# A graph network kernel: x loaded ahead of the weights, VectorE's order in the preamble changed, seven projection steps put ahead of the edge loop

## The reference, cut to what matters

```python
h = jnp.maximum(_layernorm(x, axis=-1), 0.0)          # x: 512 x 512
# layer 0, on h:
z = _ln(h, ln1_g, ln1_b)
q = (z @ Wq + bq).reshape(L, H, D)                    # L = 512 nodes, H = 8 heads, D = 64
k = (z @ Wk + bk).reshape(L, H, D)
v = (z @ Wv + bv).reshape(L, H, D)
scores = einsum('ehd,ehd->eh', q[row], k[col]) * scale + bias     # one row for each edge
m = segment_max(scores, row); p = exp(scores - m[row])
alpha = p / segment_sum(p, row)[row]
out = segment_sum(alpha[:, :, None] * v[col], row)
x = h + out.reshape(L, C) @ Wo + bo
# then a feed-forward part of the layer, and three further layers
```

## Time and profile before

| what | value |
|---|---|
| median of 3 runs | 392.35 us (392.17 to 392.61) |
| the profiled execution's own time | 392.51 us |
| its span in the profile | 391.0 us |
| TensorE busy | 371.8 us, 95% of the span |
| VectorE busy | 312.3 us, 80% |
| ScalarE busy | 171.6 us, 44% |

### The profile page before, as it was taken

One profiled execution on the slowest core, in us unless ns is written; L12 is line 12 of the kernel. 1 busy time (PEld: TensorE's weight loads), 2 busy tenths in 40 slices (PEclk: granted clock), 3 DMA queues, 4 the chain that ended last, 5 costly groups with the idle time before them and its releaser, 6 DMA issues.

```text
span 391.0 us, 5100 instructions
## 1 busy us (share of the span) xinstructions
PE 371.8 (95%) x1782; PEld 280.6 (72%) x1782; DVE 312.3 (80%) x660; ACT 171.6 (44%) x287; POOL 4.2 (1%) x19
## 2 busy tenths in 40 slices
PE   2889999999999999999989999999999999999994
PEld 2545566666657888887768788887578878787883
DVE  5889999999948689897876978499875778488356
ACT  5664665563145233343568623361363531125320
POOL 4000000000000000000000000000000000000000
PEclk9999999999999999999999999999999999999999
DMA  7602444343126000067400321400420032000002
GB/s 234 259 1 70 148 155 148 106 140 121 58 80 218 1 3 0 2 216 268 161 2 1 123 94 31 183 2 0 134 83 0 3 106 108 3 0 0 2 6 101
DMA packets 16360, 32.92 MB, mean 84 GB/s; under 512 B 1360, under 2 KB 1488, under 8 KB 16336
## 3 DMA queue, kind: packets, MB, share of 16 engines
q1 hardware_dynamic: 15744, 32.25, 24.2%
q10 hardware_dynamic: 592, 0.36, 0.4%
HBM read 21.07 MB, written 1.05 MB: 57 GB/s over the span
## 4 chain that ended last, share of the span: by engine, by line
PE 77%; DVE 14%; ACT 4%; issue 3%; DMA 1%; DVEq 0%; ACTq 0%
PE acc L1395 12%; PE bank L1377 10%; PE bank L1480 7%; PE bank L1270 6%; PE bank L1271 6%; PE bank L1251 4%; PE acc L1251 4%; PE acc L1270 4%; PE acc L1271 4%; PE bank L1465 3%; PE acc L1451 3%; DVE big_rounded L651 2%; PE acc L1228 2%; PE bank L1228 2%; PE acc L1545 2%
## 5 line engine op out<-in xcount | busy, mean ns | idle before, releaser
L1395 PE MATMUL acc<-wide_rounded,c_rounded 128*126 128x512 f32 x200 | 59.5, 439 | 0.7 <-ACT acc L463 0.7
L1395 PEld LDWEIGHTS acc<-wide_rounded,c_rounded 128*126 128x126 f32 x200 | 37.0, 187 | 19.7 <-issue 13.0
L791 DVE TENSOR_SCALAR wide_rounded<-iota_f,picked 128x512 fp32r<-128x512 f32 x100 | 42.2, 481 | 1.5 <-issue 1.1
L482 ACT COPY z_sb<-acc 126x512 f32<-126x512 f32 x37 | 21.6, 584 | 42.0 <-PE acc L1395 33.3
L506 ACT ACTIVATE wide<-wide,low_col 128x512 f32<-128x512 f32 x32 | 21.3, 716 | 32.9 <-DVE low_col L904 32.8
L624 DVE TENSOR_TENSOR wslot_rounded<-wslot,wide_rounded 128x512 fp32r<-128x512 f32 x24 | 16.2, 687 | 21.3 <-ACT wslot L376 21.3
L1480 PEld LDWEIGHTS bank<-v_sb,big 128*128 128x128 f32 x256 | 29.7, 192 | 4.7 <-issue 4.3
L1480 PE MATMUL bank<-v_sb,big 128*128 128x65 f32 x256 | 31.6, 278 | 0.0
L797 DVE TENSOR_TENSOR c_rounded<-row_bc,wslot_rounded 128x1008 fp32r<-128x1008 bf16 x25 | 30.0, 1202 | 0.0
L1377 PE MATMUL bank<-t_sb,wslot 128*128 128x512 f32 x64 | 29.5, 594 | 0.5 <-ACT t_sb L458 0.5
L651 DVE TENSOR_TENSOR big_rounded<-big,big_rounded 128x1024 fp32r<-128x1024 f32 x24 | 29.1, 1222 | 0.5
(11 more groups left out here) (310 smaller groups left out, 765.8 us busy)
## 6 DMA issues: line engine op xcount, KB each, us to landing
big<-z_sb SPq DMA_DIRECT2D x36, 252.0 KB
big<-in_w SPq DMA_DIRECT2D x4, 2048.0 KB, 7.7
x_sb<-in_x SPq DMA_DIRECT2D x8, 256.0 KB, 5.1
big<-in_w_3t SPq DMA_DIRECT2D x2, 1024.0 KB, 6.7
row_bc<-in_rows SPq DMA_DIRECT2D x7, 256.0 KB, 6.5
wslot<-in_wq SPq DMA_DIRECT2D x1, 1024.0 KB, 9.1
wslot<-in_wk SPq DMA_DIRECT2D x1, 1024.0 KB, 11.0
wslot<-in_wv SPq DMA_DIRECT2D x1, 1024.0 KB, 13.0
```

Source lines behind the costliest of these rows:

```text
L482: nc.scalar.copy(stage[0:BROWS, b % STAGES, :], a).then_inc(S["staged"], 1)
L791: nc.vector.tensor_scalar(hot_ring[:, u, k, :], iota_f[:, :], picked[:, 0, s0 + k:s0 + k + 1], None, ALU.is_equal)
L1395: last = nc.tensor.matmul(to, st_ring[:, u, 2 * k + a, :, :].rearrange("p w k -> p (w k)"), hot_ring[:, u, k, :], start=False, stop=False, ...
```

## The change

SyncE waits until the last tile of x has landed before it issues the weights. VectorE does both tiles of x moments ahead of `slot_picks`, and `ln_coefs(0)` ahead of `slot_columns`; one_hots 0 and 1 of group 0 move from ahead of the moments of h to behind them; the slot_weights of the first eight slots and one_hots 2 and 3 move from ahead of `ln_coefs(1)` to behind the z work; and between the two VectorE now evicts banks 4 and 5 of the turned z (`z_turned(2)`, `z_turned(3)`), which ScalarE did before. TensorE, behind the transposes, waits for two evictions of each of both engines and does seven Q steps ahead of the pairs of group 0; the list is 7 steps ahead of the loop, 4 behind group 0, 2 behind each of twelve groups, and 1 behind each of eleven, so that from group 12 on it has done as many as before. VectorE's evictions of Q and K follow the new list: banks 0 and 1 behind build(2), bank 2 behind build(3). The later wait counts of `t_ready` are lowered by two.

```diff
-        qkv_group = [g for g, steps in enumerate([7, 4, 3] + [2] * 10 + [1] * 10 + [0]) for _ in range(steps)]
+        qkv_group = [g for g, steps in enumerate([7, 4, 2] + [2] * 10 + [1] * 11 + [0], -1) for _ in range(steps)]
...
             for t in range(NT):
                 sp.dma_start(x_sb[:, t, :], x[t * P:(t + 1) * P, :]).then_inc(S[f"x_in{t}"], 16)
+            sp.wait_ge(S[f"x_in{NT - 1}"], 16)
             sp.dma_start(wslot[:, 0, :, :], k_major(wq)).then_inc(S["wq_in"], 16)
...
             z_turned(1)
             act.wait_ge(S["t_ready"], 2)
             clear(Z_BANKS[0])
-            z_turned(2)
-            z_turned(3)
             clear(Z_BANKS[1])
...
+            def z_turned(t):
+
+                dve.wait_ge(S["turned"], t + 1)
+                nc.vector.tensor_scalar(t_sb[:, t, :], bank[Z_BANKS[t]][:, :], colp("ln1_g", t), colp("ln1_b", t),
+                                        ALU.mult, ALU.add).then_inc(S["t_vector"], 1)
...
             x_moments(2)
+            x_moments(3)
             slot_picks(0, 0, whole)
-            x_moments(3)
+            ln_coefs(0)
             slot_columns(0, 0, whole)
-            ln_coefs(0)
             step(3, slot_masks(early), False)
+            for t in range(NT):
+                dve.wait_ge(S["h_ready"], t + 1)
+                moments(t, h_sb, "ln_var")
             dve.wait_ge(S["tables"], 7 + NT)
             one_hots(0, 0, (0, 1))
-            for t in range(NT):
-                dve.wait_ge(S["h_ready"], t + 1)
-                moments(t, h_sb, "ln_var")
-            slot_weights(3, early)
-            one_hots(0, 0, (2, 3))
             ln_coefs(1)
             for t in (0, 1):
                 ln_plain(1, t, h_sb)
+            dve.wait_ge(S["cols_in"], 16)
+            for t in (2, 3):
+                z_turned(t)
+            slot_weights(3, early)
+            one_hots(0, 0, (2, 3))
             left_sides(0, 0)
...
-                    if qkv_group[(n + 1) * NT - 1] + RING == g:
+                    if max(qkv_group[(n + 1) * NT - 1], 0) + RING == g:
                         qkv_out(n)
...
+            pe.wait_ge(S["t_ready"], 2)
+            pe.wait_ge(S["t_vector"], 2)
+            for n, after in enumerate(qkv_group):
+                if after < 0:
+                    qkv_step(n)
             for g in range(NG - 1):
                 pairs(g, g % RING, held[GROUP * (g % 2):GROUP * (g % 2 + 1)])
                 if g == 0:
-                    pe.wait_ge(S["t_ready"], NT)
-                if g == 1:
                     pe.wait_ge(S["weights_read"], 1)
```

More of the change, by code:

```diff
@@ L229, in gnn_kernel @@
             "bias_top", "bias_turned", "bias_column", "bias_spread", "bias_low", "lows_mm", "lows_ready", "weights_exp", "turned", "t_ready",
-            "x_sums", "z_scalar", "w_hi", "pick_zeros", "meets_ready", "ranks_mm", "ranks_ready", "ends_mm", "ends_ready", "rounds_ready", "slots_ready", "slots_mm",
+            "x_sums", "z_scalar", "w_hi", "pick_zeros", "meets_ready", "ranks_mm", "ranks_ready", "ends_mm", "ends_ready", "rounds_ready", "t_vector", "slots_ready", "slots_mm",
             "picks_ready", "rows_ready", "picks_mm", "weights_mm", "weights_read", "round_steps", "built", "pair_mm", "pair_steps",
@@ L833, in _ @@
             x_moments(2)
+            x_moments(3)
             slot_picks(0, 0, whole)
-            x_moments(3)
+            ln_coefs(0)
             slot_columns(0, 0, whole)
-            ln_coefs(0)
             step(3, slot_masks(early), False)
-            dve.wait_ge(S["tables"], 7 + NT)
-            one_hots(0, 0, (0, 1))
             for t in range(NT):
@@ L843, in _ @@
                 moments(t, h_sb, "ln_var")
-            slot_weights(3, early)
-            one_hots(0, 0, (2, 3))
+            dve.wait_ge(S["tables"], 7 + NT)
+            one_hots(0, 0, (0, 1))
             ln_coefs(1)
@@ L860, in _ @@
                                            ).then_inc(S["ends_ready"], 1)
-            dve.wait_ge(S["cols_in"], 16)
             dve.wait_ge(S["bv_in"], 16)
@@ L991, in _ @@
             for t in range(NT):
-                split_lo("ff_in", t, t_lo, t_at, ready=("t_ready", NT))
+                split_lo("ff_in", t, t_lo, t_at, ready=("t_ready", 2))
             weight_lo("w1_0", 3, 4)
@@ L1532, in _ @@
             product_in_parts(FF1_BANKS, weight("w1_0", NT), halves(t_at, t_lo), reads("ff_in"), "ff1_mm",
-                             group=FT, weight_lo="w1_0_lo", second=(S["t_ready"], 2 * NT), by_tile=NT,
+                             group=FT, weight_lo="w1_0_lo", second=(S["t_ready"], 2 + NT), by_tile=NT,
                              free={2: (S["rcnt_ready"], 1), 3: (S["dinv_ready"], 1)})
```

## The result

The changed kernel takes 394.12 us (median of 6 runs, 394.00 to 394.34) against 392.31 of the kernel before on the same chip: a ratio of 1.0046, interval 1.0033 to 1.0058. It is 1.8 us slower; 394.4 was forecast.

A forecast was written before the change was run, and what follows sets the result against it. Two nearly equal chains, TensorE's and VectorE's, bound the edge loop. VectorE 3.1 us late, less 0.9 of old waits and 0.2 of TensorE room, gives +2.0 and, against the median of 392.35, 394.4 us; range 391.8 to 395.5.

The forecast's parts named there:

- Two chains of equal length: Edge loop: TensorE and VectorE chains nearly equally long; VectorE's work 77.6 of 78.4 us, last pairs 0.4 after last left side.
- x first at nothing: Loads: earlier x is worth 0, and weights slipping at most 5.0 us still arrive in time, so 0.
- The gain at z: Ahead of the loop: earlier moments and coefficients let z begin at 18.35 instead of 19.46, 1.1 us gained.
- VectorE's lateness: Ahead of the loop: left_sides(0) 3.1 us late (-1.1 + 1.7 + 1.35 + 1.1), so VectorE's loop starts about 30.7.
- 0.9 to be eaten up: VectorE's loop: its old waits of 0.9 us absorb lateness first, leaving 2.2 late at its last left side.
- TensorE's gaps: Edge loop: TensorE idles near 45 and from group 14 on, released by VectorE's left side (L797).
- The end: End of the edge loop: +2.0 us.
- 0.2 of room: End of loop: TensorE had 0 to 0.4 us of room at the last left side; 0.2 was taken.
- the work behind the loop nothing: Behind the edge loop: the same work follows in the same order, so no change in time.
- The faster rival: TensorE's list alone sets the end: 391.3 us, if VectorE enters its loop at most some 0.9 + 0.2 late; 15%.
- the ring: Term from the experiments: two places for built groups; build(2) refills group 0's, each one-hot once its slot's pairs are through.
- The clock rival: TensorE's clock falls in a 1.4 us pause ahead of the seven Q steps and stays down: 397.6 us; 5%.

The follow-up runs named there:

- run 8: Changed kernel keeping only x first and VectorE's new order ahead of z; z evictions all on ScalarE, TensorE's list of before: 391.40 us, ratio 0.9974.
- run 10: Kernel before with one edit, SyncE waits for the last tile of x before issuing the weights: 392.47 us, ratio 1.0000.
- run 4: Changed kernel with all four evictions of the turned z on ScalarE again, TensorE's list as changed: 395.93 us, ratio 1.0077.
- run 5: Changed kernel with all four z evictions on ScalarE, plus 10 zero products filling TensorE's pause behind the transposes: 394.08 us, ratio 1.0041.
- run 7: Changed kernel with early slot weights, two one-hots and left side of group 0 ahead of VectorE's evictions, TensorE's pause filled: 393.55 us, ratio 1.0027.
- run 3: Changed kernel with TensorE's list of before (pairs of group 0 first), VectorE's order and evictions as changed: 395.50 us, ratio 1.0083.

## Why the prediction was right, point by point

- **Two chains of equal length.** Right, and it decided the sign. VectorE's work in its loop was put at 77.6 us; unbroken it takes 77.4 to 77.5 (the change, run 8).
- **x first at nothing.** Right (run 10). In the changed kernel, which wants Wq earlier, the first Q step is released by ScalarE's eviction and not by a DMA (row 22.82 above).
- **The gain at z.** 1.1 forecast, 1.05 measured. Right.
- **VectorE's lateness.** 3.1 forecast at the left side of group 0, 3.4 measured. The terms: gap 1.7 and 1.78; two evictions 1.35 and 1.4; some 0.13 more because this execution's edge chain began that much later (x moments at 9.31, not 9.18). Then 0.9 to be eaten up; it was 1.0.
- **TensorE's gaps.** Right in place (46.06, 86.59, 92.49), wrong in cause: I said that VectorE's left side would be the releaser. The left sides were done before the pauses began, and the pauses end with TensorE's load of block numbers, a term of 1.2 to 2.8 us that my working left out. (The list behind them thins out one group earlier than the section on the change says: two steps stand behind each of eleven groups, not twelve.) There was one pause I had not listed: at 42 the pairs of group 3 wait for a clear on ScalarE that stands behind a block's DMA (34.77 to 40.96). It does not set the end, since VectorE's loop goes on unbroken.
- **The end.** +2.0 forecast, +2.35 at the last pairs, +1.9 in the span and +1.8 in the median. I gave TensorE 0.2 of room at the last left side and it had none: the last pairs followed it by 0.24 before and by 0.28 after. I gave the work behind the loop nothing, and 0.4 came back there. That the two misses cancel is luck.
- **What I got wrong.** The faster rival's condition. I wrote that it decides where VectorE enters its loop no more than 1.1 late, as if that hung on VectorE's own list. With seven steps ahead of the pairs, build(2) waits for pairs that end some 8 us behind the first Q step (22.82 to 30.92); runs 4, 5 and 7 show that the rival could not have come true with that list, whatever VectorE did. In these runs the left side of build(2) begins 2.85 to 2.87 behind the first of those pairs (31.06 and 33.93, 29.16 and 32.01, 28.85 and 31.71). In the changed kernel the pairs begin at 28.50, so by my estimate the ring alone would have let it begin at 31.4; it began at 32.62, and VectorE's own list was the later by some 1.2 us. (The profile puts the 1.07 ahead of 31.02 down to these pairs, but the same pause stands in the kernel before as issue.) So the error cost nothing in the sum, and that too is luck.
- **The clock rival.** Rightly put low: the pause of 1.63 us left the clock at the upper level. But it was nearer than I thought: behind 2.61 and 4.01 it fell (runs 4 and 3). The Trainium skill, "TensorE: Matmul & The Clock Gate", Part 1, has the lower level as the default, to which idleness brings the clock back; these two runs agree in kind.

## What to carry to other kernels

Before starting one engine earlier, add up the work of the engine that feeds it over the same stage: where both sums are as long as the stage, only what makes both earlier is a gain, and work handed from one to the other is paid at full price. Of a step moved ahead of a producer-consumer ring, ask what the ring's producer waits for: the moved step delays it through the back door. The part of a change that helps both engines is worth running alone; here it was the faster kernel. And a pause that the profile calls issue may be a load into registers, which no busy share counts.

## What the runs showed of the hardware that was not expected

TensorE's clock fell to its lower level behind pauses of 2.61 and 4.01 us in the middle of a busy stage, with a mean of 0.83 over 20 to 30 us, and did not behind 1.63; in both cases it was back at 1.00 from 30 us on. The pause does not decide it alone: in one of the six executions of run 4 the granted clock shows no fall. Ten zero products in the pause of 2.61 us gave back 1.85 us (395.93 to 394.08), fourteen in that of 4.01 gave back 1.28 (395.50 to 394.22).

TensorE's loads of block numbers into registers took 1.2 to 2.8 us each in the loop (L1390), and four pauses of TensorE in the changed kernel end 0.4 behind the end of one. The same eviction of a bank, 128x512 with a gain and an offset, took 1.45 us for two on ScalarE and 1.53 for two on VectorE.
